# Second-pass groups begin at odd first-pass units, by fixed tables, and both bf16 parts of a turned maximum are made together

## The reference

```python
scores = jnp.einsum('bqhd,bkhd->bhqk', q, k) / d ** 0.5      # layer 0
attn = jax.nn.softmax(scores, axis=-1)
...
att = jnp.einsum('bhtd,bhsd->bhts', q, k) * (1.0 / math.sqrt(D))   # layer 1
att = att + rel_bias
att = jnp.where(causal, att, -jnp.inf)
att = jax.nn.softmax(att, axis=-1)
y = jnp.einsum('bhts,bhsd->bhtd', att, v)
```

## Time and profile before

| | us |
|---|---|
| median of 3 runs | 1036.84 |
| lowest, highest | 1033.81, 1041.83 |
| the profiled execution's own time | 1035.68 |
| its span, first to last instruction | 1033.9 |

### The profile page before, as it was taken

One profiled execution on the slowest core, in us unless ns is written; L12 is line 12 of the kernel. 1 busy time (PEld: TensorE's weight loads), 2 busy tenths in 40 slices (PEclk: granted clock), 3 DMA queues, 4 the chain that ended last, 5 costly groups with the idle time before them and its releaser, 6 DMA issues. The chain is left out here.

```text
span 1033.9 us, 22168 instructions
## 1 busy us (share of the span) xinstructions
PE 905.2 (88%) x8501; PEld 455.6 (44%) x8501; DVE 797.6 (77%) x1600; ACT 618.8 (60%) x1312; POOL 200.3 (19%) x249
## 2 busy tenths in 40 slices
PE   5689999999999997984599999999998898766788
PEld 3212222222222223883354445554445667645568
DVE  7889999999999971656797777777773587799687
ACT  3228888888888886543226777666764346433552
POOL 2202033431211120550200011102110023133221
PEclk9659999999999998996768999999999998989899
DMA  2632435433236231111635853324301000000001
GB/s 79 187 85 61 118 94 125 83 86 91 84 93 149 93 66 16 50 35 49 177 89 138 200 103 81 78 64 113 71 8 32 3 1 1 1 0 1 4 6 36
DMA packets 61782, 73.72 MB, mean 71 GB/s; under 512 B 20247, under 2 KB 45968, under 8 KB 61662
## 3 DMA queue, kind: packets, MB, share of 16 engines
q1 hardware_dynamic: 47354, 49.22, 19.5%
q0 software_dynamic: 8576, 17.86, 7.2%
q10 hardware_dynamic: 5748, 5.22, 1.6%
HBM read 44.59 MB, written 18.16 MB: 61 GB/s over the span
## 5 line engine op out<-in xcount | busy, mean ns | idle before, releaser
L1058 DVE TENSOR_REDUCE a_negmax<-a_mbank 128x1 f32<-128x1024 f32 (+4 forms) x640 | 491.4, 818 | 85.2 <-PE a_mbank L843 42.2
L1013 ACT ACTIVATE a_probs<-a_ebank 128x512 f32<-128x512 f32 (+3 forms) x896 | 439.8, 555 | 136.4 <-PE a_ebank L880 69.1
L843 PE MATMUL a_mbank<-a_moving,a_still 48*128 48x512 bf16 (+4 forms) x1280 | 260.1, 380 | 24.8 <-DVE a_ident L1020 14.3
L871 PE MATMUL a_ebank<-b_moving,b_still 50*128 50x512 bf16 (+4 forms) x1280 | 272.0, 363 | 9.6 <-ACT a_probs L1013 8.0
L894 PE MATMUL a_acc<-a_probs,a_slot_v 128*32 128x512 f32 (+3 forms) x1792 | 221.0, 566 | 1.1 <-ACT a_probs L1013 1.1
L871 PEld LDWEIGHTS a_ebank<-b_moving,b_still 58*64 58x64 bf16 (+1 forms) x1280 | 79.3, 101 | 248.3 <-ACT a_probs L1013 203.5
L843 PEld LDWEIGHTS a_mbank<-a_moving,a_still 56*64 56x64 bf16 (+1 forms) x1280 | 76.0, 104 | 94.0 <-DVE a_negmax L1058 54.3
L880 PE MATMUL a_ebank<-a_bias_b,anti 64*64 64x176 bf16 (+3 forms) x1728 | 93.0, 228 | 0.0
L880 PEld LDWEIGHTS a_ebank<-a_bias_b,anti 64*64 64x64 bf16 x1728 | 73.2, 108 | 7.6 <-issue 0.4
L851 PE MATMUL a_mbank<-bias_a,anti 64*64 64x176 bf16 (+3 forms) x576 | 64.4, 242 | 0.0
L894 PEld LDWEIGHTS a_acc<-a_probs,a_slot_v 128*32 128x32 f32 x1792 | 35.5, 108 | 57.6 <-ACT a_probs L1013 24.8
(11 more groups left out here) (389 smaller groups left out, 1102.3 us busy)
## 6 DMA issues: line engine op xcount, KB each, us to landing
a_slot_v<-vo SPq DMA_DIRECT2D x16, 512.0 KB
b_moving<-stack SPq DMA_DIRECT2D x64, 96.0 KB
b_still<-stack SPq DMA_DIRECT2D x32, 192.0 KB
a_still<-stack SPq DMA_DIRECT2D x60, 96.0 KB, 2.8
a_moving<-stack SPq DMA_DIRECT2D x60, 96.0 KB, 2.7
expert<-in_expert_rows POOLq DMA_DIRECT2D x8, 578.0 KB, 4.1
a_bias_b<-trow SPq DMA_DIRECT2D x32, 66.0 KB
stack<-expert SPq DMA_DIRECT2D x4, 384.0 KB, 2.8
```

The source lines that it names most:

```text
L843: last = nc.tensor.matmul(mbank[COLS * c:COLS * (c + 1), bank, lo - left:hi - left], S.a_still[rows, q % 2, pr, at[c]:at[c] + COLS], S.a_m ...
L871: last = nc.tensor.matmul(ebank[COLS * c:COLS * (c + 1), step % NE, lo:512], S.b_still[rows, buf, pr, at:at + COLS], S.b_moving[rows, buf, ...
L1013: nc.scalar.activation(probs[:, g % 2, j, lows[g]:512], ebank[:, step % NE, lows[g]:512], ACT.Exp).then_inc(p_full, 1)
L1058: nc.vector.tensor_reduce(to[:, at:at + 1], mbank[:, (index - 1) % NM, 0:right - left], AX.X, ALU.max, negate=True).then_inc(m_empty, 1)
```

## The change

`first_pass_starts` is gone; `STARTS` has its numbers by hand. Layer 0 begins every group one unit earlier, at odd units, so u1 now is an odd unit (jj = 1) and u2 an even one (jj = 0). Layer 1 begins them one to four units earlier (three at the quad's start), and its first quad's fifth group at 61 instead of 65. The maxima are turned one to three units earlier. On DVE `upper` and `lower` now follow the same reduction, in layer 1's second half `combine`, `upper` and `lower` all three.

```diff
-LATENCY = {False: 0.14, True: 0.16}
-EARLY = [32, 37, 42, 47, 65]
+STARTS = {False: [23 + 2 * g for g in range(17)], True: [45, 50, 55, 57, 59, 65, 70, 75, 80, 85, 89, 92, 93]}
+EARLY = [32, 37, 42, 47, 61]
...
-    COMBINE = 1 if causal else 0
-    TURN, LATE, LAST = 17 + NM, 1 + COMBINE + NM, 1 + COMBINE
+    TURN, LATE, LAST = (19, 3, 2) if causal else (18, 2, 1)
...
-    starts = first_pass_starts(units, groups, lows, causal, TURN, LATE)
+    starts = STARTS[causal]
...
                     if q and causal and use == 0:
                         combine(q - 1)
-                    if q and use == COMBINE:
+                    if q and use == 0:
                         upper(q - 1, 1)
-                    if q and use == COMBINE + 1:
                         lower(q - 1, 1)
                     if use == 16:
                         upper(q, 0)
-                    if use == 17:
                         lower(q, 0)
```

More of the change, by code:

```diff
@@ L411, in unit_columns @@
     return (512 * unit[2], min(512 * (unit[2] + 1), (unit[1] + 1) * P)) if causal else (0, SEQ)
-def first_pass_starts(units, groups, lows, causal, turn, late):
-    n = len(units)
-    cost = [0.2 + np.ptp(unit_columns(u, causal)) / 1000 for u in units]
-    total = sum(cost)
-    before = np.cumsum([0] + cost * 3) / total
-    width = np.array([512 - lo for lo in lows])
-    begun = np.concatenate([[0], np.cumsum(width) / width.sum()])
-    second = [h for h, kt in groups].index(1)
-    rows = LATENCY[causal]
-    ahead = max(before[turn] + rows, before[n + late] + rows - begun[second])
-    starts = [int(np.searchsorted(before, b + ahead - 1e-9)) for b in begun[:-1]]
-    return starts + [starts[0] + n]
 def project_tile(nc, S, layer, t, out):
```

## The result

| | kernel before | changed kernel |
|---|---|---|
| median, us | 1037.82 (4 runs, 1033.81 to 1041.83) | 1023.59 (4 runs, 1021.87 to 1023.92) |
| profiled execution, us | 1035.68 | 1021.87 |
| its span and granted clock | 1033.9, 0.932 | 1020.0, 0.928 |

The ratio is 0.986, with a 95% interval from 0.9819 to 0.990: faster by 1.4%. The medians are 14.2 us apart and the profiled executions 13.8; the forecast was 14.4.

What follows compares the result with a forecast made beforehand. Layer 0 was taken as bound by a loop through several engines, half its groups on a first-pass loop. Layer 0's -11.2, its start's -0.2 and layer 1's -3.0 sum to -14.4, from 1036.8 to 1022.4 us; range 1017 to 1036.

Steps and rivals of the forecast that it cites:

- Part 1: Layer 0: u1 and u2 exchange halves of PE's rows; the two-group loop falls from 5.02 to 4.58 us, groups to 2.39.
- the floor: Layer 0: 2.39 us as the least time of a group, set by the second pass alone.
- the exponential's loop: Layer 0: values to s3, its exponential, s2 and values again, 2.39 us a group, taking over after the change.
- Rival C: Layer 0: score 0 behind u2 makes ACT's exponentials start late; slower, 1049 us; chance 0.09.
- The turn's cost: Layer 0: each of a quad's two turns adds 0.29 us, between 0.14 and 0.44; quad 39.94.
- The opening of layer 0: Layer 0's beginning: the earlier start gives -0.2 us (0 to -1.2), and the first quad gains 1.2.
- The last quad of layer 0: Units in a few groups gain, but its last turn moves between s1 and s2: nothing in sum.
- Part 2: Upper and lower together: 0.13 us more on DVE, twice a quad, covered by idle time in both layers.
- Part 3: The earlier start: -0.2 us in layer 0, -1.2 in layer 1's first quad (gain from 0 to 2).
- Part 4: Layer 1's turns: first-half saves 0.3 to 0.5 a quad, second-half waits about 0.35 for lower; -0.7 for seven quads.
- rival D: Layer 1's second-half turn stalls 1 us instead of 0.35, seven times: +4.6, 1027 us; chance 0.07 with the forecast.
- The very last turn: Layer 1's end: it waited 0.97 for lower, now has a group more of time and waits for nothing: -1.1 us.

Runs made afterwards that it cites:

- e1: Kernel before with only layer 0's jj order swapped, so the same starts meet the other half of PE's rows: 1027.67 us, ratio 0.9904.
- e2: Changed kernel with layer 0's jj order swapped, so its units use the same halves as in the kernel before: 1036.22 us, ratio 0.998.
- e7: Changed kernel with the next group's s0 issued right behind a turn, ahead of the unit: 1024.46 us, ratio 0.9864.
- e9: Changed kernel with layer 0's turns issued right behind the values step, ahead of s3: 1018.88 us, ratio 0.9835.
- e4: Changed kernel with layer 1's second-half turn and layer 0's last turn one unit later, behind s3: 1018.16 us, ratio 0.9809.
- e5: Kernel before with only upper and lower of each bf16 part put behind one reduction: 1036.59 us, ratio 0.9985.
- e10: The changed kernel run once more, unaltered, as base of the last group: 1025.45 us, ratio 0.9878 against the kernel before.
- e12: Kernel before with only layer 0's part of the change (table, turns, bf16 parts): 1026.02 us, ratio 0.9886.
- e3: Changed kernel with layer 0's starts, turns and bf16 parts of before, leaving layer 1's part alone: 1037.31 us, ratio 1.0008.
- e6: Changed kernel with layer 0's turns moved from behind s3 to between s1 and s2: 1024.16 us, ratio 0.986.

## Why the prediction was right, and where it was off

**Part 1, the halves, was right in its mechanism.** e1 gives 40.23 a quad from the halves alone, and e2 loses it again with everything else of the change in place. Groups without a turn take the 2.39 that was read off the end of the layer, so the floor was read rightly too, and the exponential's loop is what stands there: DVE idles 0.52 ahead of its reductions, not 0.27. Rival C failed: s0 does start 0.44 behind s3 (175.60), and that costs nothing.

**The turn's cost was mis-sized.** The forecast took 0.29, between 0.14 and 0.44; it is 0.43 with units beside it. A quad is 40.23 instead of 39.94, and the six steady quads gave 8.47 instead of 10.0. The 0.14 of the row at the end was no bound for this: no unit stands there, and behind the turn comes another matmul that uses all of PE:

```profile
376.70 0.49 PE L431 MATMUL a_mbank<-heads_out,vo 128*128 128x128 f32 x2
```

e7 shows that s0's late place isn't the cause, and e9 that the turn costs 0.10 right behind the values step.

**The opening of layer 0 was taken too small.** First quad 1.78 instead of 1.2; the start 0.69 + 1.09 instead of 0.2. e1 and e2 take these apart. From the first score to the first values step it is 4.86 before, 4.35 with the halves alone (e1), 4.18 with everything but the halves (e2) and 3.76 with both, so each gives a part of the 1.09. That stretch lies at a granted clock of 0.50, where a unit's second matmul follows its first 0.43 later (71.50, 71.93 in the changed kernel) instead of 0.22. The forecast priced the pairing at full clock and in steady groups only, and gave the earlier start 0.2. The first quad takes 43.10 before, 41.88 in e1, 42.79 in e2 and 41.32 now: the halves alone give the 1.2 that was forecast, and the term that was missing is the rest's 0.3 to 0.6. The granted clock over that quad is 0.95 before and in e1, and 0.97 in e2 and in the changed kernel; that this is the reason wasn't tried. In the later traces of kernels with the new halves the first values step comes 0.7 to 2.2 us earlier than before, so the start's 1.78 isn't exact. In all, the two errors of layer 0 cancel, by luck: -11.75 against -11.4.

**The last quad of layer 0** was taken as nothing in sum, and came out 0.28 longer: its last turn between s1 and s2 costs 0.52 (3.05 against 2.53), as e4 shows, and the groups with units pay part of it back (with the turn behind s3, in e1 and e4, the quad takes 36.23).

**Part 2** costs nothing, by e5, and in layer 0 by e1 beside the changed kernel too. Under layer 1's new table the turns wait for `lower`; how much of that is the table's and how much the joined steps' isn't separated.

**Part 3 in layer 1** was off by three times: 0.40 instead of 1.2. (The new table begins layer 1's groups three to five units earlier; the fifth group of its first quad, four.) PE waited 0.23 for a reduction a little ahead of the fifth group's scores, at 529.79, so the units there set the pace at least in part; what the scores themselves wait for isn't shown by a row.

**Part 4 was right in sum and half wrong in its parts.** Behind s3 the first-half turn saves 0.45 a quad over its two groups (5.52 before, 5.07 now; 0.3 to 0.5 forecast). The second-half turn waits for `lower`, as forecast, and costs 0.15 over its two groups (5.43 before, 5.58 now), less than the 0.35. Its wait is 0.98 where it was 0.48, so 0.50 longer, but only 0.15 of that reaches the groups' time; so rival D's wait of 1 us is there, and its 4.6 us aren't. The very last turn was forecast to wait for nothing, and it waits 1.10. It moved a group later, but the last reduction moved with it: it starts at 753.25 before and 742.74 now, 1.4 us ahead of the turn (754.62, 744.19) in both, and `combine`, `upper` and `lower` follow it in a row. By `STARTS` the last unit stood one group ahead of this turn before, behind s3, and does so now. The step that failed is "it now has a group more of time". The two groups around it take 5.99 instead of 6.51: the gain is 0.52, not 1.1. The last quad's 0.44 was in no term. Layer 1's 2.8 in the trace is near the 3.0, in part by luck.

**What the sum didn't hold**: 0.97 given back between the layers. In other kernels of the study that stretch differs from that of the kernel before by -0.4 to +2.2 us, and by +0.6 and +0.7 in e3 and e5, which have layer 0 as it was; so I take it for scatter, without having tried it.

**The total.** That the medians differ by 14.2 where 14.4 was forecast is luck as well: beside the kernel before in another group, the same kernel gained 12.0 us (e10), of which layer 0 alone gives 11.5 (e12).

**Open:** why layer 1's 2.8 us don't show in whole runs. In the profiled runs of e3 and e12 its steady quads are as expected, and the stretches at a lower clock (next section) can cover the difference (2.5 us in e3's). Whether layer 1's new order makes them more likely wasn't settled: that needs many traces of each kernel.

## What to carry to other kernels

When matmuls of two streams that each use half of TensorE's rows share the engine, write down which half each instruction uses, in program order. In this kernel neighbours in different halves start together, and whether a stream begins at an odd or an even step is worth almost one per cent (e1, 9.3 us of 1037). An instruction that uses the whole array cost 0.43 us between such neighbours and 0.10 right behind another such instruction (e9). And price such an instruction from a row in which the same neighbours are there: 0.14 us without units and 0.43 with them are the same instruction. When you move a wait, look whether what it waits for moves along.

## What the runs showed of the hardware

A matmul of one row half doesn't wait for one of the other half that stands ahead of it in the program: the unit's and the score's start within 0.01 us at 175.16, and in the kernel before s0, third in the program behind s3 and u2, starts at 144.23 with s3, and u2, which shares s3's half, at 144.46. These are starts; the ends in the rows are modelled, so they say nothing on the order in which matmuls finish. A matmul behind one of its own half starts 0.22 to 0.23 us later at a clock of 1.00 (144.23, 144.46) and 0.43 later at 0.50 (71.50, 71.93). The Trainium skill ("TensorE: Matmul & The Clock Gate", section "Part 3: Packing small matmuls — row/col tiling") has them start strictly in program order; by that rule alone e1, which leaves the order of instructions as it is and changes only the halves, could still gain, so it is the row at 144.23 that speaks against the rule, as far as starts go.

A small DVE step took 2.21 us instead of 0.17 while POOL ran a TENSOR_TENSOR of 2.35 us (e2, at 335.16).

The granted clock at layer 1's opening and end differs between executions by more than layer 1's part of the change is worth. The first quad of layer 1 took 35.64 to 42.14 us over the fourteen traces, and 36.43 to 42.14 in the seven that share the changed kernel's layer 1. Its window in e6, where the clock was 1.00 throughout:

```profile
518.50:554.93 36.43, 32.81 (x625) 17.27 (x623) 30.73 (x71) 22.61 (x54) 1.22 (x2) 1.00 0.43 113
```

and in the changed kernel, first trace:

```profile
518.23:558.83 40.60, 37.68 (x626) 19.43 (x624) 30.85 (x71) 22.63 (x53) 1.23 (x2) 0.83 0.38 102
```

The last quad took 25.91 to 34.71. In e10 the clock fell from 2.4 GHz to its lower level, 1.2 GHz, right behind PE's idle 1.1 us ahead of the last turn; in the first trace of the changed kernel the same wait was followed by 1.00. The wait thus doesn't decide it alone. A change of 3 us in one layer of this kernel was told here in the steady quads of a trace, and not by six to ten whole runs (e3, e12).
